# A two-chunk Mamba block on one core: where the two norms of chunk 0 stand in the order that ScalarE and VectorE follow, and which projections TensorE runs beside them

## The reference

```python
h = patches @ W.T + b                               # (64, 10, 512)
a = layernorm(h)
# attn part, residual stream a
x = rmsnorm(a, rms1_w)
z, xv, B, C, dt_in = split(x @ in_proj_w.T)
dt = softplus(dt_in @ dt_proj_w.T + dt_proj_b)
state = exp(dt * A) * state + (dt * x_full) * B     # scan over the 10 tokens, 16 states per channel
y = (sum_n C * state + D_skip * x_full) * silu(z)
a = a + y @ out_proj_w.T
h = h + a + mlp(rmsnorm(a, rms2_w))                 # silu(gate) * up, then down, 2048 hidden
h = h + ffn(layernorm(h))                           # the same form, other weights
```

## Time and profile before

| | |
|---|---|
| median of 3 runs | 675.78 us (672.87 to 676.73) |
| the profiled execution's own time | 675.06 us |
| its span (first to last instruction) | 673.3 us |
| TensorE busy, of the span | 631.5 us, 94% |
| VectorE, ScalarE, GpSimd busy | 418.0, 346.4, 429.2 us |
| mean granted TensorE clock | 0.98 of 2.4 GHz |

### The profile page before, as it was taken

One profiled execution on the slowest core, in us unless ns is written; L12 is line 12 of the kernel. 1 busy time (PEld: TensorE's weight loads), 2 busy tenths in 40 slices (PEclk: granted clock), 3 DMA queues, 4 the chain that ended last, 5 costly groups with the idle time before them and its releaser, 6 DMA issues.

```text
span 673.3 us, 8617 instructions
## 1 busy us (share of the span) xinstructions
PE 631.5 (94%) x2846; PEld 505.7 (75%) x2846; DVE 418.0 (62%) x532; ACT 346.4 (51%) x773; POOL 429.2 (64%) x244
## 2 busy tenths in 40 slices
PE   4969998799999989999979999999999999999998
PEld 3736765466665757777747777766999998999998
DVE  4077896889887879889887888851322223332132
ACT  4359889358989364434356433422542442653441
POOL 0176785437786999987877987644455463445461
PEclk9879998799999989999989999999999999999999
DMA  8699997489999969988866898533443453134421
GB/s 340 238 365 364 318 299 268 141 258 357 350 373 348 390 250 349 413 336 318 320 247 257 320 330 323 191 125 122 138 149 126 125 157 126 63 130 132 146 67 44
DMA packets 49164, 163.50 MB, mean 243 GB/s; under 512 B 4320, under 2 KB 18528, under 8 KB 48480
## 3 DMA queue, kind: packets, MB, share of 16 engines
q1 hardware_dynamic: 49120, 162.95, 68.9%
HBM read 145.24 MB, written 17.69 MB: 242 GB/s over the span
## 4 chain that ended last, share of the span: by engine, by line
PE 75%; DVE 11%; ACT 5%; POOL 3%; issue 3%; DMA 2%; SPq 0%; DVEq 0%; ACTq 0%; POOLq 0%
PE work L992 54%; PE da L992 15%; DVE da L784 6%; PE work L1002 5%; DVE hs L794 3%; POOL hs L447 2%; ACT L522 2%; ACT da L548 1%; DMA bb<-b_rows 1%; DMA c_rows<-c_rows 1%; DMA sm<-small 0%; POOL hs L460 0%; DVE a L849 0%; ACT z L665 0%; DVE work L809 0%
## 5 line engine op out<-in xcount | busy, mean ns | idle before, releaser
L784 DVE TENSOR_TENSOR_SCAN da<-da,hs 128x580 f32<-128x580 f32 (+1 forms) x128 | 191.1, 1493 | 39.6 <-POOL hs L447 22.2
L447 POOL TENSOR_TENSOR hs<-dtx,bb 128x1160 f32<-128x1160 f32 (+1 forms) x64 | 171.2, 2677 | 61.1 <-PE work L1002 54.1
L426 POOL TENSOR_TENSOR ws<-wraw,ws 128x1024 fp32r<-128x1024 f32 x40 | 101.4, 2536 | 92.8 <-ACT ws L557 92.8
L992 PE MATMUL work<-sq,wraw 128*128 128x290 f32 x512 | 125.7, 406 | 1.1 <-DVE sq L882 1.1
L992 PE MATMUL work<-hn,win 128*128 128x290 f32 (+1 forms) x336 | 104.4, 459 | 16.6 <-DVE hn L857 8.1
L992 PEld LDWEIGHTS work<-sq,wraw 128*128 128x128 f32 x512 | 96.5, 189 | 30.0 <-issue 1.6
L548 ACT ACTIVATE da<-dt,a_neg 128x261 f32<-128x261 f32 (+1 forms) x256 | 118.2, 493 | 0.0
L794 DVE TENSOR_TENSOR hs<-da,cb 128x580 f32<-128x580 f32 (+1 forms) x128 | 105.2, 822 | 10.7 <-DMA cb<-c_rows 2.7
L992 PEld LDWEIGHTS work<-hn,win 128*128 128x128 f32 x336 | 65.5, 200 | 50.7 <-issue 26.0
L545 ACT COPY da<-zeros 128x58 f32<-128x58 f32 (+1 forms) x128 | 27.6, 216 | 126.0 <-DVE hs L794 125.8
L557 ACT CAST ws<-wraw 128x1024 fp32r<-128x1024 f32 x48 | 50.3, 1048 | 70.2 <-PE da L992 34.4
(11 more groups left out here) (98 smaller groups left out, 655.2 us busy)
## 6 DMA issues: line engine op xcount, KB each, us to landing
wraw<-w_stream SPq DMA_DIRECT2D x104, 512.0 KB, 4.1
bb<-b_rows SPq DMA_DIRECT2D x32, 700.0 KB, 7.1
cb<-c_rows SPq DMA_DIRECT2D x32, 700.0 KB, 5.6
bb<-b_rows SPq DMA_DIRECT2D x32, 580.0 KB, 8.0
cb<-c_rows SPq DMA_DIRECT2D x32, 580.0 KB, 6.0
c_rows<-c_rows SPq DMA_DIRECT2D x8, 875.0 KB, 10.8
c_rows<-c_rows SPq DMA_DIRECT2D x8, 725.0 KB, 6.6
win<-w_in SPq DMA_DIRECT2D x4, 1024.0 KB, 13.4
```

Source lines behind the costliest of these rows:

```text
L426: nc.gpsimd.tensor_tensor(ws[:, k % NW, 1, :], wraw[:, split_loads[k] % NRAW, :], ws[:, k % NW, 0, :].bitcast(F32), ALU.subtract).then_inc ...
L447: nc.gpsimd.tensor_tensor(hs[:, u % NH, 0:NQ * n].rearrange("p (n t) -> p n t", t=n), dtx[:, t % 2, 0:n].unsqueeze(1).to_broadcast([P, NQ, ...
L784: nc.vector.tensor_tensor_scan(da[:, j, 0:w], da[:, j, 0:w], hs[:, u % NH, j * w:(j + 1) * w], 0.0, ALU.mult, ALU.add).then_inc(scan_done, 1)
L992: last = nc.tensor.matmul(dst, w, x, start=(k == 0), stop=(k == len(pairs) - 1))
```

## The change

The order of steps is changed; no arithmetic is, and no instruction is added. One table load is dropped.

- TensorE: projection `in_z` of tile 6 (chunk 1) runs in slot 31 instead of slot 37; `in_c` of tile 6 goes from slot 32 to slot 36; `in_z` of tile 7 from slot 50 to 37; `dtp` of tile 7 from slot 51 to 50; `in_c` of tile 7 from slot 36 to 51.
- ScalarE: the squares of `rms2` stand in slot 36 behind the first-half decays of unit 37; its logarithm and exponential stand in slot 37 ahead of the first-half decays of unit 38. For the layer norm, squares, logarithm and exponential all stand in slot 50, ahead of the first-half decays of unit 51.
- VectorE: a table `PLACE` gives each of the norm's steps a place among the scan's parts of its slot.
- SyncE: the store of C rows of tile 6 goes from slot 35 to 39, that of tile 7 from slot 39 to 54.

```diff
     bg += two_tiles(1, 0) + two_tiles(1, 2) + two_tiles(1, 4)
+    bg[-1].append(("in_z", 1, 6))
...
-    first = [[("dtp", 1, 6), ("in_c", 1, 6), ("xs", 1, 6)], [("xs", 1, 7)], o[0:2], o[2:4]]
+    first = [[("dtp", 1, 6), ("xs", 1, 6)], [("xs", 1, 7)], o[0:2], o[2:4]]
...
-        rest += {"rms2": [("in_c", 1, 7), s, ("in_z", 1, 6)], "ln2_mean": [s, ("in_z", 1, 7)],
-                 "ln2_var": [s, ("dtp", 1, 7)]}.get(s[0], [s])
+        rest += {"rms2": [("in_c", 1, 6), s, ("in_z", 1, 7)], "ln2_mean": [s, ("dtp", 1, 7)],
+                 "ln2_var": [s, ("in_c", 1, 7)]}.get(s[0], [s])
...
-SEAM = (("in_c", 1, 7), ("in_z", 1, 6), ("in_z", 1, 7), ("dtp", 1, 7))
+SEAM = (("in_c", 1, 6), ("in_z", 1, 7), ("dtp", 1, 7), ("in_c", 1, 7))
+
+PLACE = {("out", 0, 2): 2, ("out", 0, 3): 2, ("rms2", 0): 2, ("ln2_mean", 0): 1, ("ln2_var", 0): 0}
...
-                    norm = [s for s in steps if s[0] in ("rms2", "ln2_var")]
-                    if norm:
-
-                        n = steps.index(norm[0])
-                        between = [steps[n - 1]] if steps[n - 1] == SEAM[2] else []
-                        first = steps[:n - len(between)] + [("squares",) + norm[0]]
-                        second = between + [("root",) + norm[0]] + steps[n + 1:]
+
+                    if i + 1 < len(slots) and ("rms2", 0) in slots[i + 1][1]:
+                        second.insert(0, ("squares", "rms2", 0))
+                    if ("rms2", 0) in steps:
+                        first, second = [("root", "rms2", 0)], [s for s in steps if s[0] != "rms2"]
+                    if ("ln2_mean", 0) in steps:
+                        first = [("squares", "ln2_var", 0), ("root", "ln2_var", 0)]
+                        second = [s for s in steps if s[0] != "ln2_mean"]
+                    if ("ln2_var", 0) in steps:
+                        first, second = [], [s for s in steps if s[0] != "ln2_var"]
...
+                    for s in reversed([s for s in others if s in PLACE]):
+                        parts.insert(PLACE[s], s)
+                    others = [s for s in others if s not in PLACE]
```

More of the change, by code:

```diff
@@ L706, in step @@
                             gated_high(i)
-            for unit, steps in late(slots, 1):
+            for i, (unit, steps) in enumerate(late(slots, 1)):
                 if unit == 0:
```

## The result

The median of 17 runs fell from 675.78 to 671.82 us; the ratio to the runs before is 0.9934, with a 95% interval of 0.9915 to 0.9953. By the ratio that is 4.5 us less (3.2 to 5.7), and by the two medians 4.0, where 6.8 were forecast. The ratio leaves out one run of each kernel that lies far off: 3666.94 us before, and 815.51 us after, at a granted clock of 0.752. The profiled execution of the changed kernel took 673.53 us (span 671.7), the slowest of the other 16.

The account below looks back on a forecast made before the run. The prediction took TensorE to bound chunk 0's MLPs, leaving 13.3 us of idle or slow places. Terms 4.0 + 2.8 = 6.8 us took the profiled 675.06 to 668.3; with the median 0.7 higher, 669.0 us, range 665.0 to 672.8.

Parts of the forecast that it names:

- the 5 to 9 of the forecast: Whole kernel: the forecast outcome of 5 to 9 us gained, given chance 0.55.
- The layer norm: Second MLP's start: `gu` starts 6.9 us earlier, most paid back through the tanh and banks; term 2.8 us.
- The tenth product: Second MLP: TensorE's tenth product goes into the bank `gate_y` frees, with slack 0.3 us, which counts towards the 2.8 us.
- rms2 with the stretch ahead of it: Slots 31 to 36 and the first MLP's start: `gu` starts 5.1 us earlier, 4.0 us left at the third product.
- `out` starts 0.7 us earlier.: Ahead of `rms2`: `gate_y` had waited 0.69 us for TensorE and is now met by it, so `out` starts earlier.
- The removed 1.65 us of low clock at the norm's product: At `rms2`: without the 2.97 us wait, the norm's product runs at full clock, saving 1.65 us.
- What follows `out`: From `out` to the first MLP's third product: unit 36 about 0.5 us earlier, that product at 245.75 instead of 249.73.
- The wait at the third product: First MLP: TensorE waits about 1 us for the bank that `gate_y` frees, wanted at 244.6 and free at 245.7.
- banks and scan keep up: Rival, chance 0.12: both earlier `gu` starts survive in full, 12.0 us gained, time 663.8 us.
- ScalarE's queue is the pace: Rival, chance 0.15: each us of tanh later than 356.5 is paid in full; with doubled table loads, time 671.6 us.
- The store of C rows: SyncE, tile 7: store in slot 54, load in slot 58, four units of 7.85 us later; costed at nothing.
- GpSimd's earlier softplus: Tile 7: softplus on GpSimd one unit earlier, its result first used in unit 60; costed at nothing.

Follow-up runs that it names:

- e3: The changed kernel with the first tanh of the second MLP moved ahead of the second-half decays of unit 52; median 669.42 us, ratio 0.9911.
- e4: The changed kernel with two more table loads ahead of the first tanh of the second MLP; median 674.06 us, ratio 0.9978.
- e1: The changed kernel with the layer norm's steps on ScalarE and VectorE placed as before, rms2 and projections as changed; median 676.16 us, ratio 1.0013.
- e9: The kernel before with the burst of weight loads split, the last two at `in_z` of tile 5; median 675.29 us, ratio 1.0010.
- e6: The changed kernel with four weight loads of `out` at `in_z` of tile 2 and two at `in_z` of tile 6; median 669.39 us, ratio 0.9921.
- e8: The changed kernel with both the early first tanh and the split weight loads; median 667.46 us, ratio 0.9895.
- e5: The changed kernel with `in_c` of tile 6 in slot 32, that of tile 7 in slot 36, none in slot 51; median 670.74 us, ratio 0.9946.
- e7: The changed kernel with early first tanh, one more projection ahead of `out` and split weight loads together; median 668.61 us, ratio 0.9917.

## Why the prediction was right, and where it was off

Direction and range held (671.82 in 665.0 to 672.8). The size came out at two thirds. The narrower statements did not hold: 4.5 us is just below the 5 to 9 of the forecast and the 4.6 us to which its terms' bounds add up. One term was right to 0.1 us and the other a quarter of its size, below its own bound of 3.4; that the sum still fell into the range is in part luck.

**The layer norm, forecast 2.8 us: measured 2.7 to 2.9** (D 108.74 to 108.89 before, 106.04 after). Every piece stands in the profile: wait 0.83 us, squares' product at full clock, first tanh 2.6 us earlier relative to the mean's product (16.79 against 19.42) and 8.8 behind the first product of `gu` (forecast 9). That product starts 8.02 us behind the mean's, against 14.89 before: 6.87 us, of which 4.1 are paid back. The timeline shows 1.76 + 0.34 + 0.85 = 2.95 us of it as waits; about 0.5 more is inside the long group behind them (nine products in 366.19 to 384.30, 18.11 us, where nine take 17.6), and the rest in ends of groups. The tenth product was not alone in setting the gain: the eighth, at 366.19, waits 0.85 us for `times_gate`. e3 and e4 move the first `times_gate`, counted from the mean's product, by -1.53 us (353.02 - 337.32 against 358.05 - 340.82) and by +2.58 (358.42 - 338.61), and D follows by -1.55 and +2.88. So the first tanh's place in ScalarE's queue is the pace. e1 shows that the gain is the placement's: without it the same projections lose 2.0 us against before.

**rms2 with the stretch ahead of it, forecast 4.0 us: measured about 1.0.** This is the mis-sized term: A+B+C is 46.83 us in the mean of the four profiles that have the change's program there (after, e1, e3, e4) and 47.85 in that of the three of before (47.59 with e9, which would make it 0.8). Three steps of the working failed, and one nearly held.
- *"`out` starts 0.7 us earlier."* TensorE was ready about 1.3 us earlier, but A went from 17.3 to 17.6 in the mean. I read the wait of 0.69 us for TensorE ahead of `gate_y` as the whole slack, and took the landing of unit 33's C rows from one profile; it was the earliest of the nine profiles without the split preload (12.1 to 14.0 us behind the mark). e6 takes 1 MB out of the queues, and A falls to 16.12, below my 16.6.
- *That `out` runs at full clock* was not even stated. It ran at the lower level in all five profiles whose preload and projections are the change's: 1.6 us in B.
- *The removed 1.65 us of low clock at the norm's product* is there in two profiles of before and absent in the second and in e9. A cost that half the profiles do not have is worth about half.
- *What follows `out`* held up to 0.6 us, where `out` runs at full clock. The forecast had unit 36's scan about 0.5 us earlier, at 231.5 (30.1 us behind the mark), and the third product at 245.75, 14.3 us behind it. e6 and e8 have that scan 30.1 us behind the mark and the product 14.8 us behind the scan; 0.50 us of the difference is a wait of the scan that follows the scaling (row 247.10 of the change, the same in e6 and e8), which the working had left out. So with the C rows early the term is 3.0 us (47.85 - 44.88), or 3.5 against the first profile of before, from which the 4.0 were worked. In the change itself the late and slow `out` is the limit instead, and takes 2 us of that. The wait at the third product is 1.08 us (forecast 1.1).

The sum of the two terms as measured, 1.0 + 2.8 = 3.8 us, lies within the interval of 3.2 to 5.7.

Of the rivals, "banks and scan keep up" is refuted by the bank waits. "ScalarE's queue is the pace" was right as a mechanism, as e4 shows, but already contained in the forecast's 2.8 us. The store of C rows and GpSimd's earlier softplus cost nothing that shows.

## What to carry to other kernels

When work is moved so that an engine arrives earlier somewhere, look at everything that the next step waits for, with its spread over several profiles; the wait that was covered becomes the limit (here C rows, 12.1 to 14.0 us behind the same mark). A seam's gain must be followed to the shared buffers behind it and to what frees them: 6.9 us at the MLP's start were worth 2.8, since the tanh that starts the freeing of banks came only 2.6 us earlier. And when the pace-setting instruction is known, move that: one tanh ahead of two decays gave 1.55 us, more than the whole rework of `rms2` gave with the C rows late.

## What the runs showed of the hardware

Idle time ahead of a group did not alone decide TensorE's clock. Ahead of `out`, waits of 1.50 (e4), 1.63, 2.24, 2.43 and 2.71 us were all followed by the lower level. Ahead of the product of `rms2`, 2.97 and 3.03 us were (3.76 and 3.67 us for it), but 2.82 and 2.98 us were not (2.19 us). At the layer norm e5 and e7 have the same wait of 2.29 us ahead of the same products; e5 then runs at the lower level and e7 doesn't (0.50 and 1.00 in the windows). e4's wait of 4.34 us was followed by it. So no fixed price can be put on a wait from one profile; and in e4, where VectorE is busy 94% of the windows at the lower level, that level cost 0.3 us at most.

In the kernel before, a C-row load of chunk 1 takes 5.6 us in the median and 10 to 15 us around the burst of six weight loads. Two loads of 512 KB fewer in the burst (e6) took the wait of unit 33 from 2.3 us to nothing, though the loads there still took 9.3 to 13.7 us.
